# Two reorderings in TensorE's queue of a windowed-attention block: the probabilities' turn between two halves of the scores, and the output projection ahead of the keys' projection

## The reference, cut to what matters

```
def attn_layer(x, Wqkv, qs, ksc, Wo):
    q, k, v = split_heads(x @ Wqkv)
    q, k = l2norm(q) * qs, l2norm(k) * ksc
    q = q * cos * scale + rotate_half(q) * sin * scale
    k = k * cos / scale + rotate_half(k) * sin / scale
    sim = (q of a window) @ (k of it and the one before).T * 8, masked
    attn = softmax(sim, -1)
    return (attn @ v) @ Wo
x = attn_layer(shift_tokens(x), ...) + x
x = ffn_layer(shift_tokens(x), ...) + x      # layer norm, gated GELU
```

## Time and profile before

| | us |
|---|---|
| runs of the kernel before | 4337.57 (median), 4336.9, 4341.59 |
| the profiled execution's own time | 4342.59 |
| span of its trace | 4340.8 |
| PE busy | 4033.6 (93%) |
| DVE busy | 3357.6 (77%) |
| POOL busy | 2965.1 (68%) |
| ACT busy | 2587.4 (60%) |
| mean granted clock of PE | 0.967 |

### The profile page before, as it was taken

One profiled execution on the slowest core, in us unless ns is written; L12 is line 12 of the kernel. 1 busy time (PEld: TensorE's weight loads), 2 busy tenths in 40 slices (PEclk: granted clock), 3 DMA queues, 4 the chain that ended last, 5 costly groups with the idle time before them and its releaser, 6 DMA issues. The chain is left out here.

```text
span 4340.8 us, 151604 instructions
## 1 busy us (share of the span) xinstructions
PE 4033.6 (93%) x66856; PEld 2965.1 (68%) x66856; DVE 3357.6 (77%) x3997; ACT 2587.4 (60%) x3022; POOL 2965.1 (68%) x3501
## 2 busy tenths in 40 slices
PE   8989969999999999999968888799999999999997
PEld 5655557877777777887633332577877887777775
DVE  5635568887888888888658884689888888887885
ACT  4424436666666667666527775367666666666664
POOL 2202158988888888888524441688888888888884
PEclk9999989999999999999969997899999999999999
DMA  4304233233233323322100000332323333232221
GB/s 150 124 10 143 105 94 82 75 88 82 75 88 80 83 78 84 90 69 74 40 11 1 1 1 1 105 86 78 85 78 85 88 84 87 72 88 78 73 67 38
DMA packets 169726, 316.94 MB, mean 73 GB/s; under 512 B 39336, under 2 KB 43056, under 8 KB 166640
## 3 DMA queue, kind: packets, MB, share of 16 engines
q1 hardware_dynamic: 153520, 241.18, 20.5%
q0 software_dynamic: 15552, 66.07, 4.9%
HBM read 92.03 MB, written 20.05 MB: 26 GB/s over the span
## 5 line engine op out<-in xcount | busy, mean ns | idle before, releaser
L684 PE MATMUL psum<-loc_w_hl,loc_z_lo 128*128 128x512 f32 x1152 | 508.5, 441 | 36.1 <-DMA loc_w_hl<-parted 25.9
L1069 POOL TENSOR_TENSOR loc_rc_k<-loc_rc_k,loc_rs_k 128x1024 f32<-128x1024 f32 x192 | 454.5, 2367 | 18.9 <-DVE loc_rs_k L1197 18.9
L1183 DVE TENSOR_REDUCE loc_ssq<-loc_sq 128x16 f32<-128x1024 f32 x384 | 463.9, 1208 | 3.4 <-POOL loc_rn L1065 3.3
L930 ACT ACTIVATE loc_sq<-psum 128x1024 f32<-128x1024 f32 x192 | 197.0, 1026 | 444.1 <-PE psum L686 439.0
L1069 POOL TENSOR_TENSOR loc_rc_q<-loc_rc_q,loc_rs_q 128x1024 f32<-128x1024 f32 x192 | 459.3, 2392 | 0.0
L686 PE MATMUL psum<-loc_w_hl,loc_z_hi 128*128 128x512 f32 x1152 | 455.3, 395 | 1.8 <-issue 1.8
L685 PE MATMUL psum<-loc_w_hl,loc_z_hi 128*128 128x512 f32 x1152 | 454.3, 394 | 2.5 <-issue 2.5
L1087 POOL TENSOR_TENSOR loc_prob<-loc_prob,loc_recip 128x1024 f32<-128x1024 f32 x192 | 365.9, 1906 | 97.2 <-DVE loc_recip L1220 96.6
L781 PE MATMUL psum<-loc_PT,loc_V 64*64 64x32 f32 x24576 | 404.8, 220 | 10.4 <-issue 10.2
L781 PEld LDWEIGHTS psum<-loc_PT,loc_V 64*64 64x64 f32 x24576 | 381.2, 135 | 35.6 <-issue 12.4
L801 PEld LDWEIGHTS psum<-loc_outT,loc_wo 128*128 128x128 f32 x3072 | 378.5, 194 | 17.8 <-issue 1.5
(11 more groups left out here) (199 smaller groups left out, 9753.3 us busy)
## 6 DMA issues: line engine op xcount, KB each, us to landing
loc_V<-loc_V SPq DMA_DIRECT2D x1152, 128.0 KB
loc_V<-loc_V SPq DMA_DIRECT2D x672, 64.0 KB
loc_w_hl<-parted POOLq DMA_DIRECT2D x72, 512.0 KB, 4.3
parted<-moe_halves POOLq DMA_DIRECT2D x18, 1024.0 KB, 5.2
moe_spread<-moe_gates SPq DMA_DIRECT2D x64, 256.0 KB, 4.1
moe_raw<-in_wqkv POOLq DMA_DIRECT2D x18, 512.0 KB, 6.0
moe_w<-in_moe_w SPq DMA_DIRECT2D x32, 256.0 KB, 3.3
loc_wo<-in_wo SPq DMA_DIRECT2D x12, 512.0 KB, 4.8
```

The lines of the kernel that those rows point to most:

```text
L684: pe.matmul(M.bank[bank + g], z_lo[:, r, tokens], w[:, 0, cols], start=True, stop=False)
L1069: pool.tensor_tensor(rc, rc, rs[:, :], ALU.add).then_inc(added, 1)
L1183: dve.tensor_reduce(ssq[:, a:a + HEADS], heads(sq[:, :]), AX_X, ALU.add).then_inc(totalled, 1)
```

## The change

In PE's queue alone, and in its order alone:

- `scores` becomes two functions. `mask_scores` has the waits and the two matmuls of the mask, `scores(L, t, first, end)` runs a range of the eight head pairs; the semaphore for DVE is raised at the end of the second half, as before.
- `turn_probs` of tile n-2, which stood ahead of the mask and all scores of tile n-1, now stands between the first four head pairs and the last four.
- `output` of tile n-4 now stands ahead of `project_k` of tile n.

```diff
@@ -739,7 +739,7 @@
-            def scores(L, t):
+            def mask_scores(L, t):
                 i = t % TILES
                 pe.wait_ge(qT_ready, upto(L, t))
                 for c in range(2):
@@ -748,13 +748,17 @@
                 pe.wait_ge(kT_ready, upto(L, t))
                 pe.sem_inc(pe_passed, 1)
-                for p in range(PAIRS):
+
+            def scores(L, t, first, end):
+                i = t % TILES
+                for p in range(first, end):
                     for w in range(TILES):
                         for c in range(2):
...
-                mm.then_inc(s_full, 1)
+                if end == PAIRS:
+                    mm.then_inc(s_full, 1)
@@ -861,10 +865,10 @@
                 newest = n - 4 if live(n - 4) else -1
+                if live(n - 4):
+                    output(L, n - 4)
                 if live(n):
                     project_k(L, n, live(n - 3))
-                if live(n - 4):
-                    output(L, n - 4)
@@ -893,10 +897,13 @@
+                if live(n - 1):
+                    mask_scores(L, n - 1)
+                    scores(L, n - 1, 0, PAIRS // 2)
                 if live(n - 2):
                     turn_probs(L, n - 2, live(n - 1))
                 if live(n - 1):
-                    scores(L, n - 1)
+                    scores(L, n - 1, PAIRS // 2, PAIRS)
```

## The result

| | us | ratio to before, 95% interval |
|---|---|---|
| before, median of 4 | 4337.23 (4332.78 to 4341.59) | |
| after, median of 4 | 4520.83 (4506.27 to 4533.28) | 1.0425 [1.0398, 1.0453] |
| profiled execution of after | 4533.28, span 4531.2 | |

The change makes the kernel slower by 183.6 us at the medians, 190.7 us between the two profiled executions (4342.59 to 4533.28). The forecast was +218 for these. The granted clock is the same in both (0.967 over the span), and in the two local blocks it is 0.99 and 1.00 before and 0.99 and 0.99 after, the 2.4 GHz level. So the clock has next to no part in the difference. Lines of PE's queue have shifted by 3 or 4 (scores 758, values 785, output 805, variance 818, last 862), those of ACT, DVE and POOL by 7.

A forecast was written before the change was run, and what follows sets the result against it. The prediction took PE, 96% busy in the two local blocks, as the bound. Waits +230, tile-size changes +38 and stalls -50 gave +218 us: 4560.6 us profiled, 4556 us median (+5.0%), range 4450 to 4650.

The forecast's parts named there:

- ACT's copy to outT stopped waiting: Sign in the changed profile: this copy's 164.8 us of waiting for the values' matmuls falls to a quarter.
- The query projection waits for outT at n % 4 = 3 and 0: Query projection, no room: ACT's copy to outT ends later, so it waits 1.4 us in each of these steps.
- n % 4 = 2: Mask in these steps: ACT's run from outT through copy of v delays qT, costing 1.25 us.
- n % 4 = 1: Mask in these steps: it waits for qT, after ACT's extra affine of the norm, costing 0.95 us.
- This part costs nothing: Moving the output projection first was to cost nothing at n % 4 = 1, where no table load occurs.
- the 230 forecast: Waits from both reorderings, 5.0 us per four steps in 46 groups: +230 us, bounds 200 to 260.
- More changes between tile sizes: Two more changes between small and full tiles on PE, 0.2 us in each of 192 steps: +38 us.
- Stalls in the scores nearly go: Stalls in the scores, read as waits for instructions, fall from 52 us to about 12: -40 us.
- stalls stay: Rival: stalls in the scores remain or only move to the second half; +268, 4606 us, chance 0.10.
- The stalls in the values: Most stalls in the values fall ahead of the query projection's new wait: -10 us.
- 46 groups: Groups of four steps having all their parts; the blocks' first steps, with no output yet, were left out.
- Other engines have room: DVE's and POOL's later work was to leave room at the key turn; POOL's sum is 13.7 us of 17.

The follow-up runs named there:

- out_first: The kernel before with only the output projection moved ahead of the keys' projection, scores and turn as they were: 4457.79 us, ratio 1.0300.
- split26_not1: The kernel before with the turn behind two of eight head pairs, but ahead of mask and scores at n % 4 = 1: 4369.71 us, ratio 1.0096.
- after_again: The changed kernel itself, run again as base line on the chip of later runs: 4513.41 us, ratio 1.0433.
- before_noload: The kernel before with GELU replaced by the identity in the local blocks, so no table reloads: 4319.35 us, ratio 0.9986.
- after_z: The changed kernel with DVE adding the attention (output projection of tile n-4) first in its step: 4512.77 us, ratio 1.0428.
- after_noload: The changed kernel with GELU replaced by the identity in the local blocks, so no table reloads: 4431.43 us, ratio 1.0238.
- after_noload_z: The changed kernel without GELU and its table reloads, and with DVE adding the attention first in its step: 4359.93 us, ratio 1.0074.
- split_only: The kernel before with only mask and first half of the scores ahead of the turn, output projection where it was: 4442.68 us, ratio 1.0263.

## Why the prediction was right, and where its steps were off

Sign, size (+5.0% forecast, +4.25% measured) and the main mechanism held. That the sum came within 27 us of the 191 is partly luck. The waits were 44 us too large in it; cutting the scores cost 7 us more than it had, the stalls in scores and values saved some 26 us less, and it lacked two things, other irregular time (-33 us) and the first steps of the blocks (+15 us). Of the signs that it named, ACT's copy to outT stopped waiting (164.8 to 6.4 us), the step is 17.1 us long on average, and no new wait for DVE or POOL stands at the key or query turn; the stalls in the scores did not fall to 12 us. Point by point:

- **The query projection waits for outT at n % 4 = 3 and 0.** Right; 1.11 and 1.16 us instead of 1.4. Three sizes were off. ACT's next instruction starts 0.97 us after the exponential's start (1238.68 to 1239.65), not at its end 1.06 after, and the copy is a little shorter (1.00 instead of 1.03); so the copy's end moved by 1.24, not 1.4. The Trainium skill, page "ScalarE: Activation LUTs", section "What ACT_TABLE_LOAD costs", has neighbouring ACTIVATEs overlap by 93 ns; these rows agree, with 0.09 us. Then I took the projection's start at 1209.39 to have no room, though outT was ready at 1209.06: in after it starts 0.06 us behind outT, so 0.27 of the 0.33 was room. That leaves 0.97. And a projection that starts behind a wait takes longer itself: from its first matmul to the next section's it is 1.49 us (1240.71 to 1242.20) instead of 1.36 (1209.39 to the next section at 1210.75), which makes the 1.11.
- **n % 4 = 2.** Right in place (through copy of v), 0.88 instead of 1.25. The wait falls at the queries' turn, which needs copy of v; qT then follows in time, and nothing more is lost at the mask.
- **n % 4 = 1.** The mask waits for qT: 0.89 instead of 0.95. "This part costs nothing" there was wrong for the swap alone: 0.55 us for POOL (out_first). The split's wait covers it, so the sum was right.
- Sum of these: 4.04 us per four steps, not 5.0: 46 x 0.96 = 44 us less than the 230 forecast. This is most of the miss.
- **More changes between tile sizes.** 0.25 us a step by regular lengths instead of 0.2 (after), 0.27 in the three kinds that split26_not1 cuts. That is 45 us in 46 groups for the 38 forecast. The term was the sum of the two changes' 0.1; the turn's own eight matmuls being 0.15 slower between small tiles was not in it.
- **Stalls in the scores nearly go.** Wrong. Gaps over 0.15 us between the starts of successive instructions in the scores beyond the regular ones: 45 with 53.0 us before, 40 with 42.4 us in after, 37 with 37.9 in after_again. All 45 of before lie behind the middle of the section; all 40 of after lie in its second half, behind the turn. The stall moved, it didn't vanish: -11 to -15 us and not -40. Even that much is not clear of chance: before_noload, with PE's order of before, has 35 with 38.7 us. The rival "stalls stay" was nearer for this term. The rule of the Trainium skill that stood behind that rival ("Runtime: NRT & Kernel Launch", "Instruction fetch mechanics": the fetch is hidden) is another matter; the last section has what the traces show of it. The stalls in the values did go (22 with 15.0 us to 5 with 1.8, -13, forecast -10), and in three of four steps they now fall ahead of a wait.
- Part of this error was made up by other irregular time, which the forecast did not have. The whole irregular part fell by 1.24 us per four steps, 57 us in 46 groups, where I had forecast 50 from the scores and values alone. By sections it fell by 0.15 in turn, mask and scores, by 0.37 in the values, and by 0.72 (33 us) in all the others. I read this as small pauses that fall ahead of a new regular wait and are hidden by it; no run isolates it.
- **46 groups.** The first steps of the blocks were left out, since they have no output yet. But the split makes the mask wait for qT there too, 12 us.
- **Other engines have room.** It held for the changed kernel (after_z moved nothing), but this was luck: DVE's addition to zs came just as late as outT, no later. I checked the key turn behind the sine product and not who waits for the addition behind it. Where ACT is faster, that addition costs 71 us (after_noload against after_noload_z). The copy to PT was not in the working either. It costs nothing here (0.7 us in 2 matmul gaps, against 45.4 in 134 in split_only) only because the output projection stands in front of the keys' projection.
- The sum with the measured terms: 46 x (4.04 + 0.98 - 1.24) = 174 us for the groups, near the 176 counted; with 15 us outside them, 12 of them the mask's first waits, about the 190.7 between the profiled executions.

Not settled: why the turn is 0.15 us slower between small tiles (the weight loads' order or the change of tile size), why the scores of before take 1.5 us in three of four kinds and 1.41 in the fourth, and what part of the stalls' difference is chance, since their count differs from trace to trace (35 and 45 with the same order of PE).

## What to carry over

Before an in-order engine's sections trade places, write down for each section not only what it waits for but what every other queue does once it ends, and follow all of these chains to where they come back: here one came back through ACT (outT), one as long through DVE (zs), one through POOL (the probabilities), and where two chains were equally long, the profile named only one. Room between two neighbours, in time for a copy to empty a bank, is a resource: a cut that halves the work behind a turn spends it. Two parts of a change must be measured alone and together, since 131 and 116 us made 184.

## What the runs showed of the hardware

Leaving GELU out of the kernel before took away 132 of the 133 table loads for the exponential and all 134 for GELU, 1.28 us each, and moved its time by -0.14% [-0.37, +0.09]. The next ACTIVATE starts 0.01 us behind a load (1237.39 + 1.28 and 1238.68). The Trainium skill, page "ScalarE: Activation LUTs", section "What ACT_TABLE_LOAD costs", counts 2.66 us for a switch, with a drain; no drain shows in these rows, since ACT's squares directly ahead end as the load begins.

The stalls in dense small matmuls follow the instruction queue closely. The stall of 1.20 us above that ends at 1284.62 has one packet of q8 in its past; the DMA queues of after from 1282.2 to 1283.2 us show it (packets, MB, share of 16 engines):

```profile
q8 instruction: 1, 0.02, 5.5%
```

It starts at 1282.25, and PE resumes 2.37 us later. Over all stalls above 0.4 us in the scores and values PE resumes 2.2 to 3.0 us after the start of a q8 packet, median 2.53 in before and 2.56 in after, and 1.2 to 1.6 us after the packet has landed. In the local blocks of before a packet starts every 6.3 us on average, so a random moment would lie in that range of 0.8 us one time in eight. The count of packets, 529, is the same in both kernels. This fits waiting for instructions, which would be hidden where PE waits for another engine and show in whichever half of the scores it falls; no run here took the fetching away, so it is not shown beyond this coincidence.
